# A graph network on one core: the first six loads of counts issued in another order, and a wait per tile

## What is computed

```
x = x + segment_sum(edge_weight * (sigmoid(h@Wg+bg) * (h@W))[dst], src)     # layer 0
x = x + segment_sum(h[src], dst) @ W1.T + b1                                # layer 1
x = x + update(h, segment_sum(messages(h[src], h[dst]), dst))               # layer 2
x = x + relu(batchnorm(Dinv * sum(Binv * sum((h@W3)[row])) + b3))           # layer 3
```

## Time and profile before

| | us |
|---|---|
| median of 3 runs | 2562.01 |
| lowest, highest | 2561.71, 2567.41 |
| the profiled execution | 2568.25 |
| its span | 2566.4 |
| TensorE busy | 2309.7 (90%) |
| VectorE busy | 1596.8 (62%) |
| ScalarE busy | 1181.9 (46%) |

### The profile page before, as it was taken

The page is one execution under the profiler, slowest core; times in us unless marked ns, Lnnn a source line. Parts: engine busy times, 40 slices in busy tenths (PEclk is TensorE's granted clock), DMA queues, the critical chain, the costliest instruction groups (busy, mean ns, idle before and its releaser), DMA issues.

```text
span 2566.4 us, 70830 instructions
## 1 busy us (share of the span) xinstructions
PE 2309.7 (90%) x27901; PEld 1990.4 (78%) x27901; DVE 1596.8 (62%) x3655; ACT 1181.9 (46%) x2490; POOL 46.3 (2%) x52
## 2 busy tenths in 40 slices
PE   3489999999899998999939999899998999999997
PEld 2368878887787887877838888788887888887886
DVE  8689999999999998999962333234333112122223
ACT  3488778877777876888831222122221000011112
POOL 3300000000000000000000000000000000000000
PEclk9599999999999998999979999999998999999998
DMA  7589999999999999999989999999997999999998
GB/s 197 119 166 220 208 209 210 219 210 207 209 186 221 207 203 193 204 218 214 217 197 228 290 289 290 262 260 259 257 258 204 290 289 290 273 245 244 261 266 193
DMA packets 1608984, 589.35 MB, mean 230 GB/s; under 512 B 964422, under 2 KB 1605450, under 8 KB 1608567
## 3 DMA queue, kind: packets, MB, share of 16 engines
q1 hardware_dynamic: 1604869, 579.88, 101.8%
q0 software_dynamic: 1600, 4.92, 0.7%
q10 hardware_dynamic: 2226, 0.62, 0.2%
HBM read 255.26 MB, written 89.20 MB: 134 GB/s over the span
## 4 chain that ended last, share of the span: by engine, by line
PE 49%; SPq 22%; DMA 11%; DVE 6%; issue 5%; ACT 5%; POOL 1%; DVEq 0%; ACTq 0%; POOLq 0%
PE ps L676 33%; SPq L419 13%; SPq L446 8%; DMA counts_by_source<-stage 7%; PE ps L589 2%; ACT stage L1208 2%; PE ps L591 2%; PE ps L590 2%; ACT stage L1193 2%; DVE X L924 2%; PE ps L614 2%; DMA a_turned<-counts_by_source 2%; PE ps L615 2%; PE ps L616 2%; PE ps L597 1%
## 5 line engine op out<-in xcount | busy, mean ns | idle before, releaser
L1208 ACT CAST stage<-ps 128x784 f16<-128x784 f32 x784 | 655.7, 836 | 105.5 <-DMA counts_by_source<-stage 73.3
L676 PE MATMUL ps<-Ha,a_tiles 128*128 128x258 f16 x4606 | 523.8, 273 | 6.9 <-DVE Ha L994 6.9
L614 PE MATMUL ps<-hot_c,hot_r 128*128 128x98 f16 x3136 | 508.2, 211 | 14.1 <-DVE hot_c L912 7.5
L676 PEld LDWEIGHTS ps<-Ha,a_tiles 128*128 128x128 f16 x4606 | 449.9, 98 | 73.4 <-DVE Ha L994 7.6
L615 PE MATMUL ps<-hot_c,hot_r 128*128 128x98 f16 x3136 | 502.1, 210 | 0.0
L616 PE MATMUL ps<-hot_c,hot_r 128*128 128x98 f16 x3136 | 500.4, 210 | 0.0
L589 PE MATMUL ps<-g_in,wt 128*128 128x128 f16 x2401 | 431.5, 222 | 38.1 <-DVE X L924 21.7
L1193 ACT CAST stage<-ps 128x392 f16<-128x392 f32 x784 | 398.3, 508 | 141.9 <-PE ps L597 141.9
L590 PE MATMUL ps<-g_in,wt 128*128 128x128 f16 x2401 | 429.7, 222 | 0.0
L591 PE MATMUL ps<-g_in,wt 128*128 128x128 f16 x2401 | 429.6, 222 | 0.0
L924 DVE SCALAR_TENSOR_TENSOR X<-ps,X 128x512 f32<-128x512 f32 (+1 forms) x637 | 392.1, 649 | 45.5 <-PE ps L591 45.3
(11 more groups left out here) (195 smaller groups left out, 2029.9 us busy)
## 6 DMA issues: line engine op xcount, KB each, us to landing
a_tiles<-counts_by_source SPq DMA_DIRECT2D x147, 1600.0 KB, 13.7
counts_by_source<-stage SPq DMA_DIRECT2D x49, 1600.0 KB, 8.1
gated_parts<-G SPq DMA_DIRECT2D x7, 448.0 KB, 3.6
g_in<-gated_parts SPq DMA_DIRECT2D x98, 32.0 KB, 3.1
out_x<-X SPq DMA_DIRECT2D x12, 256.0 KB
edge_table<-tab SPq DMA_DIRECT2D x1, 2448.0 KB, 10.4
wt<-stage SPq DMA_TRANSPOSE x98, 10.9
dst_run<-in_dst SPq DMA_DIRECT2D x1, 612.4 KB
```

The lines of the kernel that those rows point to most:

```text
L614: mm(into(0), rows_, codes(0), start=v == 0, stop=True, skip_group_check=True)
L676: last = mm(ps[:, sum_bank(ph, j, c), 0:PARTS], a_slot(ph, c, i), moving[:, i], start=i == 0, stop=i == TILES - 1)
L1208: a.copy(stage[:, b, 0:2, 0:TILES, u * SET_COLS:(u + 1) * SET_COLS], of).then_inc(s("hi_done"), 1)
```

## The change

SyncE issues the first six loads of pass 1 in another order and behind other waits. Behind the last `hand_on` it waits for both buffers' stores except tile 48's and for the transposes out of buffer 1, and issues the loads of tiles 3 and 4. Then it waits for tile 48's store (`counts_stored`) and its transposes (`wt_in0`), and issues the loads of tiles 0, 1 and 2. Then it waits for all additions and issues the load of tile 5. The loop of pass 1 issues the loads from tile 6 on, as before. In `first_tiles` TensorE waits for each tile's load ahead of that tile's part of portion 0, in the order 3, 0, 1, 2, which all portions now take; `sum_done1` rises by four once, behind the last portion of tile 2.

```diff
@@ SyncE, behind the building loop
                 tiles_loop(sp, hand_on, 0)
+
+                def load_counts(ph, j, c):
+
+                    q = load_at(ph, c) % SLOTS
+                    sp.dma_start(a_tiles[:, q].rearrange("p (i a) d -> p i (a d)", a=2), two_tiles(j)).then_inc(s(f"a_in{q}"), 16)
+
+                sp.wait_ge(s("stored1"), 16 * (TILES // 2))
+                sp.wait_ge(s("stored0"), 16 * (TILES // 2))
+                sp.wait_ge(s("wt_in1"), 32 * (TILES // 2))
+                for j in (3, 4):
+                    load_counts(1, j, j)
                 counts_stored(sp)
+                sp.wait_ge(s("wt_in0"), 32 * GROUPS)
+                for j in (0, 1, 2):
+                    load_counts(1, j, j)
                 sp.wait_ge(s("added"), FOURS * TILES)
+                load_counts(1, 5, 5)
 
                 for ph in (1, 2, 3, 4):
 
                     def step(j, k, c, ph=ph):
-                        if not on(j):
+                        if not on(j) or (ph == 1 and not later(j, SLOTS)):
                             return
-                        q = load_at(ph, c) % SLOTS
...
-                            sp.dma_start(a_tiles[:, q].rearrange("p (i a) d -> p i (a d)", a=2), two_tiles(j)).then_inc(s(f"a_in{q}"), 16)
+                            load_counts(ph, j, c)
@@ TensorE, pass 1
                     def first_tiles():
 
-                        for j in range(TOGETHER):
-                            pe.wait_ge(s(f"a_in{load_at(1, j) % SLOTS}"), (load_at(1, j) // SLOTS + 1) * 16)
                         for part in range(SET):
                             pe.wait_ge(s("h_ready1"), part + 1)
-                            for j in range(TOGETHER):
+                            for j in (3, 0, 1, 2):
+                                if part == 0:
+                                    pe.wait_ge(s(f"a_in{load_at(1, j) % SLOTS}"), (load_at(1, j) // SLOTS + 1) * 16)
                                 for i in range(part * SET, (part + 1) * SET):
                                     last = mm(ps[:, sum_bank(1, j, j), 0:PARTS], a_slot(1, j, i), Ha[:, i], start=i == 0, stop=i == TILES - 1, skip_group_check=True)
-                                if part == SET - 1:
-                                    last.then_inc(s("sum_done1"), 1)
+                                if part == SET - 1 and j == 2:
+                                    last.then_inc(s("sum_done1"), TOGETHER)
```

## The result

The changed kernel takes 2549.8 us at the median of 6 runs (2546.3 to 2553.5), the one before 2562.6: ratio 0.9948, 95% interval 0.9934 to 0.9961. That is 12.8 us less, and by the interval 10 to 17 us. One of the six runs of the kernel before took 5785.3 us and is left out of the ratio, as is one of 12638.1 us in a later comparison; without it the kernel before has a median of 2562.3.

The account below looks back on a forecast made before the run. At the start of pass 1, TensorE's 27.5 us wait for the first four tiles' loads was taken as the bound. 12.4 us gained less 0.9 for the later signal gives 11.5: from 2562.01 to 2550.5 us, range 2545.7 to 2558.0.

Parts of the forecast that it names:

- TensorE's start: First matmul of pass 1's first four tiles: at 1327.9, 17 us earlier, once Ha's first portion is there.
- The last load wanted: Tile 2's load, fifth in a queue of 5.65 us each, lands at 1335.1; TensorE pauses 2.7 us for it.
- The clock: Behind the pause for tile 2: 5.4 us at 1.2 GHz, then the other 149.6 of 175 matmuls in 16.7 us.
- The early-clock rival: TensorE's clock rises despite the pause for tile 2, 175 matmuls take 19.5 us: gain 14.0, 2548.0 us; chance 0.21.
- The last transpose: Tile 48's last transpose shares at most its last 1.2 us with the early loads: priced 0 to 1 us, taken as 0.
- The late signal: One rise of sum_done1 at the four tiles' end delays tile 4's start: 0.9 us lost, bounds 0 and 1.0.
- The additions beside the traffic: VectorE's last additions now run beside the loads: 0.69 us each with traffic, 0.68 without; nothing taken.
- What follows: From tile 4 on, the passes shift as a block and the gain stays; load 6 costs nothing.
- the queue with holes: 1.5 us holes ahead of loads 3, 0 and 2 bring tile 2 in 4.5 us later: 2555.0 us; chance 0.13.
- Loads 3 and 4 did start early: Rival denied here: a semaphore or SyncE holds loads 3 and 4 until 1319.4; 2563 to 2566 us, chance 0.04.
- the clock did not stay down: Rival denied here: TensorE stays at 1.2 GHz through the first four tiles; 3.7 us slower, 2565.7 us, chance 0.04.
- the queue was no faster than forecast: Rival denied here: at 436 GB/s a load takes 3.8 us, none holds TensorE; gain 16.3, 2545.7 us, chance 0.02.

Follow-up runs that it names:

- the second comparison: The changed kernel, unaltered, measured once more beside the kernel before: 2554.8 us, ratio 0.9972.
- the warm clock: 180 matmuls with unread results ahead of TensorE's wait for Ha's first portion, added to the kernel with load order 3, 0, 1, 2, 4, 5 and one signal a tile: 2543.8 us.
- the order alone: The changed kernel with only tile 4's load moved behind those of tiles 0, 1 and 2: 2541.2 us, ratio 0.9927.
- the waits alone: The kernel before with only TensorE's wait for each tile's load moved ahead of that tile's first portion, loads issued as before: 2558.2 us, ratio 0.9983.

## Why the prediction was right

The forecast was 2550.5 us and 11.5 us gained, range 2545.7 to 2558.0; 2549.8 us and 12.8 us were measured, and 10.0 us in the stage itself. Its steps, each put on the mark (1301.17 before):

**TensorE's start:** 1327.9, or 26.7 from the mark, right to 0.1 us. Ha's first portion releases it.

**The last load wanted:** 33.9 forecast, 35.9 measured. The mechanism is right (TensorE is held at tile 2), the term is 1.9 us too small, which makes a pause of 4.7 us out of 2.7, and a pause of 0.5 us ahead of it, at tile 1, that I did not have. I let five loads follow the store's landing at 5.65 us each, as if nothing were lost at the handover. The landings, in us from the mark, show where it was lost:

| landing | forecast | measured |
|---|---|---|
| store of tile 48 | 5.7 | 6.6 |
| tile 3 | 11.3 | 12.9 |
| tile 4 | 17.0 | 18.5 |
| tile 0 | 22.6 | 24.6 |
| tile 1 | 28.3 | 30.2 |
| tile 2 | 33.9 | 35.9 |

The store itself lands 0.9 us later than I had it:

```profile
counts_by_source<-stage SPq DMA_DIRECT2D x1, 1600.0 KB, 8.3
```

It takes 8.3 us in all kernels that issue a load right behind it, and 7.5 in the one that waits for its landing first. Tile 3's load then needs 6.4 us behind the store, which is 0.7 too much, and tile 0's, the first behind SyncE's wait for the store, 6.05, which is 0.4 too much; the other three take 5.6 to 5.7. Where the store ends and the loads begin, the traffic falls to 180 GB/s for 2.2 us, which is (1 - 180 / 290) x 2.2 = 0.8 us of the 1.9. The dip lies ahead of the store's landing, so I did not separate how it divides between the first two rows.

**The clock:** here the two cases that I named were not all. I had it either rise behind the pause, after 5.4 us, or rise before its end and stay. It rose 2.8 us behind the first matmul, before the pause, then fell within it and rose again 3.8 us behind its end. In the change's second execution it rose in the pause itself, 0.1 us behind its start, fell again before its end, and rose 3.0 us behind it. (In the execution with one signal a tile it took the forecast's way: no rise before the pause, and one 3.3 us behind it.) The 175 matmuls took 21.5 us, forecast 22.1 (5.4 + 16.7): 0.6 us too much, which hid part of the load's error. The early-clock rival (19.5 us) had its early rise and failed all the same, since the clock did not stay up. That the pause was longer than I had it doesn't explain this: the clock fell 1.7 us into it, and I had 2.7 us for the whole. The rule of the Trainium skill that I set beside it ("TensorE: Matmul & The Clock Gate", section "HAM oscillation — how this bites in real kernels"), that a pause for a DMA makes the warm-up be paid again, agrees with these windows: 0.99 before the pause, 0.50 behind it. The case in that section has waits of about 3 to 5 us, though, and the pause that I set beside it was 2.7; the measured ones are 4.7 and 4.0.

**The last transpose:** I took nothing for its sharing with the loads, and it is nothing: with the loads behind it, it takes 9.9 to 10.0 us in every kernel, before 9.87 and 9.96.

**The late signal:** 0.9 forecast, 1.0 measured in two pairs of kernels.

**The additions beside the traffic:** taken at nothing, and it is. In the changed kernel's timeline of VectorE they still take 0.67 to 0.69 us each and start 1.37 us apart, and Ha's first portion comes at 26.7 from the mark in every kernel with the waits, whether loads run beside them or not.

**What follows:** shifts as a block, right; load 6 is not waited for.

The sum by steps in the stage: 58.5 forecast, 60.0 measured, which is 1.9 too little for the load, 0.6 too much for the clock and 0.1 too little for the signal. Of the rivals, the queue with holes was right in kind (a loss at the handover) and too large in size: 4.5 us against 1.9. Loads 3 and 4 did start early (issued from 1.1 us ahead of the mark on), the clock did not stay down, and the queue was no faster than forecast, so the other three fell. The stage gave 1.5 us less than the forecast's 11.5 and the whole time 1.3 us more. That the whole time lies on the other side is owed to the spread of the building, and no merit of the sum; the second comparison, 0.9972 or some 7 us, lies below the forecast. And the load's error would have shown more but for the clock's, which went the other way.

## What to carry to other kernels

When several loads have to be in before an engine runs on, the place of the last one wanted in the queue sets the time, one load's duration for each place, as long as the engine is held by it. Issue first exactly what is wanted first: here tile 4's load, second in the queue and wanted last of the five, cost 7 us, while the head start over the store was worth half a us to one. For a change of 10 us in a kernel whose executions spread by 10, count from an event just ahead of the change to one just behind it, and let the whole time only confirm it.

The fastest version by the stage is the one with the loads in the order 3, 0, 1, 2, 4, 5, one signal a tile and the warm clock (51.4 us against 70.0); by the whole time it can't be told from the one with the order alone (0.9924 and 0.9927). Both lie below the change's 0.9948 and 0.9972, though their intervals still overlap that of the first.

## What the runs showed of the hardware

The granted clock's rise behind a restart is not a fixed time. In the eight executions where it rose before any long pause, or in its first 0.2 us, I read 2.8 to 5.7 us from the first matmul of the four tiles to the rise, and the same kernel gave 5.7 and 4.6 (before), 2.8 and 5.3 (the change). Nor does a rise last: in the change's two executions TensorE went idle 1.7 us behind the rise and 0.1 us ahead of it, and the clock fell again 1.7 and 3.6 us into the pause for tile 2. Each us at the lower level costs the stage about half a us (3.2 and 5.2 us at it, 23.60 and 24.52 us for the 196 matmuls of the two kernels with the other order), so two executions of one stage can differ by about a us for this alone.

Where the store is followed by loads in one queue, the traffic dips to 160 to 200 GB/s for two us, in the change and in the kernel with the other order. From an idle queue, in the kernel with the waits alone, hardly anything moves in the first 1.1 us behind the issue, and 178 GB/s in the us after that. A store of 1600 KB that takes 7.4 to 7.5 us with nothing of its size behind it takes 8.3 with a load behind it. Most of the 10 us by which whole executions of this kernel differ arise in the building, before the stage: the last store of counts is issued anywhere from 1289.9 to 1299.5 us, while what follows tile 4 differs by 3.2 us.
